# VectorE's mixing operations placed between the masked copies of a scan step, and the state's decay product moved to the middle of the step

## What is computed

```python
sx = concatenate([zeros_like(x[:, :1]), x[:, :-1]], axis=1) - x
m = tanh((x + sx * time_maa_x) @ tm_w1).reshape(Bb, Tt, 5, A)
delta = einsum('btfa,fac->btfc', m, tm_w2)
mix = time_maa_wkvrg[None, None] + delta
xw, xk, xv, xr, xg = [x + sx * mix[:, :, i] for i in range(5)]
...
def step(state, rkvw):
    a = k_t[..., :, None] * v_t[..., None, :]
    y = einsum('bhk,bhkv->bhv', r_t, state + u[None, :, :, None] * a)
    return (w_t[..., :, None] * state + a, y)
...
return yn.reshape(Bb, Tt, Cc) * g @ Wo
```

## Time and profile before

| | us |
|---|---|
| device time, median of 3 runs | 4354.51 (4353.13 to 4363.64) |
| span of the profiled execution, first to last instruction | 4344.3 |
| what lies around the span (median less span) | 10.2 |
| attention | from the start to about 2640 |
| TensorE busy / VectorE busy / ScalarE busy / GpSimd busy | 3769.6 / 3500.5 / 1612.9 / 1139.1 |

### The profile page before, as it was taken

How to read it: one execution, slowest core, us unless ns; L and a number is a source line. 1 busy time by engine, 2 the same in 40 slices (tenths; PEclk the granted TensorE clock), 3 DMA queues, 4 the chain that set the end, 5 groups by cost and what they waited for, 6 DMA issues and landing times. The chain is left out here.

```text
span 4344.3 us, 155632 instructions
## 1 busy us (share of the span) xinstructions
PE 3769.6 (87%) x65992; PEld 2590.6 (60%) x65992; DVE 3500.5 (81%) x7798; ACT 1612.9 (37%) x3173; POOL 1139.1 (26%) x736
## 2 busy tenths in 40 slices
PE   4888898888898888888888874399999999999999
PEld 3767777676677766777767652145454545545454
DVE  4777788777688776778777757799999999999997
ACT  2434434344353443443434313233333333333333
POOL 1121112211212212112121104433333333333332
PEclk7999999999899998999999986599999999999999
DMA  3000000000000000000000011001111111111100
GB/s 112 13 22 27 23 28 18 23 27 18 23 27 23 27 22 19 27 18 33 18 23 27 13 71 66 15 23 37 31 37 35 33 38 30 37 32 36 38 30 30
DMA packets 73617, 133.45 MB, mean 31 GB/s; under 512 B 13248, under 2 KB 14016, under 8 KB 72896
## 3 DMA queue, kind: packets, MB, share of 16 engines
q1 hardware_dynamic: 72896, 123.13, 8.8%
HBM read 89.56 MB, written 33.55 MB: 28 GB/s over the span
## 5 line engine op out<-in xcount | busy, mean ns | idle before, releaser
L747 POOL TENSOR_TENSOR raw_up<-raw_up,raw_gate 128x1024 f32<-128x1024 f32 x128 | 309.8, 2420 | 1184.1 <-DVE raw_up L797 1184.1
L915 DVE COPY_PREDICATED Am<-pick,banks 128x64 f32<-128x64 uint8 (+2 forms) x1792 | 460.6, 257 | 128.3 <-DVE Am L915 12.6
L1630 PE MATMUL fbank<-dT,hqT 128*128 128x512 f16 x2112 | 490.3, 381 | 21.1 <-ACT hqT L1547 21.1
L1618 PE MATMUL fbank<-gT,xqT 128*128 128x464 f16 (+1 forms) x2304 | 490.1, 363 | 11.4 <-issue 6.6
L1618 PE MATMUL fbank<-uT,xqT 128*128 128x464 f16 (+1 forms) x2304 | 488.3, 362 | 0.0
L526 PE MATMUL banks<-raw_up,raw_gate 128*128 128x256 f32 x2048 | 465.8, 386 | 6.2 <-issue 4.4
L526 PEld LDWEIGHTS banks<-raw_up,raw_gate 128*128 128x128 f32 x2048 | 391.0, 193 | 61.0 <-issue 7.0
L758 POOL TENSOR_TENSOR yrs<-yvar,neg_half 128x32 f32<-128x32 f32 x32 | 174.0, 5437 | 846.0 <-DVE yvar L944 846.0
L1618 PEld LDWEIGHTS fbank<-gT,xqT 128*128 128x128 f16 x2304 | 225.3, 98 | 247.7 <-issue 11.5
L1558 ACT ACTIVATE sil<-fbank,und 128x464 f32<-128x464 f32 (+1 forms) x192 | 124.0, 646 | 656.0 <-PE fbank L1618 656.0
L1618 PEld LDWEIGHTS fbank<-uT,xqT 128*128 128x128 f16 x2304 | 225.6, 98 | 231.7 <-issue 1.3
(11 more groups left out here) (235 smaller groups left out, 8063.1 us busy)
## 6 DMA issues: line engine op xcount, KB each, us to landing
raw_scale<-in_L_attn_x SPq DMA_DIRECT2D x32, 512.0 KB, 3.8
xres<-in_L_attn_x SPq DMA_DIRECT2D x32, 512.0 KB, 3.5
x_after_attention<-xres SPq DMA_DIRECT2D x32, 512.0 KB, 3.6
xl<-x_after_attention SPq DMA_DIRECT2D x64, 256.0 KB, 2.7
xr<-x_after_attention SPq DMA_DIRECT2D x64, 256.0 KB, 2.7
out<-xr SPq DMA_DIRECT2D x64, 256.0 KB, 2.0
raw_gate<-in_L_ffn_w_gate SPq DMA_DIRECT2D x1, 2816.0 KB, 11.5
raw_up<-in_L_ffn_w_up SPq DMA_DIRECT2D x1, 2816.0 KB, 18.7
```

The lines of the kernel that those rows point to most:

```text
L747: nc.gpsimd.tensor_tensor(xf[:, j % NXF].rearrange("p g b t -> p (g b) t"), xf[:, j % NXF].rearrange("p g b t -> p (g b) t"), hT[:, :, :, ...
L915: nc.vector.copy_predicated(dst, mask, src).then_inc((done or A_step).sem, 1)
L1618: last = nc.tensor.matmul(GU[2 * pair + t][:, 0:w], xqT[:, u, a, g, :], W[:, b_, g, lo_:hi_], start=(k == 0), stop=(k == 3 * G - 1))
L1630: last = nc.tensor.matmul(DN[1 - u][:], hqT[:, a, kk, :], dT[:, b_, kk, :], start=(first and kk == 0), stop=(end and kk == KF - 1))
```

## The change

Two things are done to VectorE's instructions of a scan step.

1. The four mixing operations of steps 1 to 5, which stood together behind the seven masked copies, now stand one by one inside the step: the first behind the fourth copy, the second behind the update of the state, the third behind the sixth copy, the last behind the seventh. The waits of the mixing (for `delta` and for a free `xf`) stand ahead of the first of them, so inside the step. What followed the four (for `j = 0` the addition of `hT`) is now `dve_mix_end`, and it is called ahead of `dve_z`; before, `dve_z` stood ahead of the whole mixing.
2. The product `s_tmp = state * decay` moves from behind the diagonal product to behind the third copy, in all eight steps.

```diff
-        def dve_mix(dve, i, j):
-            after(dve, delta_done, i, j + 1)
...
+        def dve_mix(dve, i, j, g):
+            if g == 0:
+                after(dve, delta_done, i, j + 1)
...
+            part = nc.vector.scalar_tensor_tensor(xf[:, j % NXF, g], PROJ[g // 2][:, (g % 2) * BT:(g % 2 + 1) * BT].rearrange("p (b t) -> p b t", b=B),
+                                                  col_maa[:, ORDER[j], g:g + 1], sx[:, g], ALU.add, ALU.mult)
+            if g == G - 1:
+                part.then_inc(mixed.sem, 1)
+
+        def dve_mix_end(dve, i, j):
             if j == 0:
                 after(dve, mixed, i, 1)
...
-        def dve_A(dve, c, n):
+        def dve_A(dve, c, n, mix):
...
+            level(16, 4, M1, M2)
+            level(16, 8, M2, M3)
+            level(16, 12, M3, X0)
             if q == 0:
                 after(dve, state_done, c - 1, 4 * b + 4)
             else:
                 after(dve, state_done, c, n)
             nc.vector.tensor_tensor(s_tmp[:], state[:, b, q], t32, ALU.mult).then_inc(s_step.sem, 1)
...
             level(32, 16, X0, SEND)
+            mix(0)
             level(4, 1, S1, S2)
             after(dve, s_step, c, n + 1)
             nc.vector.tensor_tensor(state[:, b, (q + 1) % Q], s_tmp[:], SC[n % 2][:, G * NS:G * NS + G * K].rearrange("p (g v) -> p g v", g=G), ALU.add).then_inc(state_done.sem, 1)
+            mix(1)
             level(4, 2, S2, S3)
+            mix(2)
             level(4, 3, S3, M1, A_done)
+            mix(3)
...
                 if do_w:
-                    dve_A(dve, c, n)
+                    dve_A(dve, c, n, mix)
...
+                if 1 <= n <= 5 and do_p:
+                    dve_mix_end(dve, i, n - 1)
                 if n == 1 and do_f:
                     dve_z(dve, f)
...
-                if 1 <= n <= 5 and do_p:
-                    dve_mix(dve, i, n - 1)
```

More of the change, by code:

```diff
@@ L788, in dve_m @@
             nc.vector.tensor_tensor(m_part[1][:, 1, 0:QT], m_full[:, 1, 0:QT], m_hi[:, 1, 0:QT], ALU.subtract).then_inc(m_done.sem, 1)
-        def dve_mix(dve, i, j):
-            after(dve, delta_done, i, j + 1)
[L792 to L799, removed]
+        def dve_mix(dve, i, j, g):
+            if g == 0:
+                after(dve, delta_done, i, j + 1)
+                if j == 0:
+                    after(dve, td1_done, i - 1)
+                else:
+                    after(dve, proj_done, i - 1, 2 * j)
+            part = nc.vector.scalar_tensor_tensor(xf[:, j % NXF, g], PROJ[g // 2][:, (g % 2) * BT:(g % 2 + 1) * BT].rearrange("p (b t) -> p b t", b=B),
[3 more added lines that the diff above has]
+        def dve_mix_end(dve, i, j):
             if j == 0:
@@ L904, in dve_A @@
             t32 = T32[:].rearrange("p (g x) -> p g x", g=G)[:, :, xb:xb + 1].to_broadcast([P, G, K])
[L905 to L909, removed]
             step = [1]
@@ L927, in dve_A @@
             level(16, 12, M3, X0)
+            if q == 0:
+                after(dve, state_done, c - 1, 4 * b + 4)
+            else:
+                after(dve, state_done, c, n)
+            nc.vector.tensor_tensor(s_tmp[:], state[:, b, q], t32, ALU.mult).then_inc(s_step.sem, 1)
             level(32, 16, X0, SEND)
+            mix(0)
             level(4, 1, S1, S2)
@@ L968, in dve_body, with mix @@
             for n in range(8):
+                def mix(g):
+                    if 1 <= n <= 5 and do_p:
+                        dve_mix(dve, i, n - 1, g)
                 if do_w:
-                    dve_A(dve, c, n)
+                    dve_A(dve, c, n, mix)
+                else:
+                    for g in range(G):
+                        mix(g)
+                if 1 <= n <= 5 and do_p:
+                    dve_mix_end(dve, i, n - 1)
                 if n == 1 and do_f:
```

## The result

The changed kernel takes 4508.07 us (median of 4 runs, 4499.32 to 4514.88) against 4353.82 (4350.05 to 4363.64): 3.66% slower, ratio 1.0366 with a 95% interval of 1.0333 to 1.0399. The forecast was 4495, in a range of 4435 to 4540.

What follows compares the result with a forecast made beforehand. The prediction took TensorE's own stream as the bound, with g(1) repeatedly delayed by another engine. To 4354.5 us it added 105 (chain), 6 (later last copy) and 30 (clock), 141 in all: 4495 us, range 4435 to 4540.

Steps and rivals of the forecast that it cites:

- What bounds the kernel: In the attention TensorE's own stream sets the pace; only at g(1) does another engine repeatedly delay it, 15.7 us in all.
- The chain through `dve_z`: Step 1: `dve_z` behind the mixing makes g(1) start 6.1 us after delta(0) ends, against 2.6; +105 us.
- The later last copy in steps 2 to 5: Last masked copy stands behind three mixing operations, so TensorE's output starts later: +6 us, range 0 to 18.
- The decay product as a cushion: Moved product keeps the last copies of steps 3 and 4 in time; without it 0.5 to 1 us a body lost.
- The clock: g(1)'s products meet TensorE's lower clock after the wait in about two thirds of bodies: +30 us, range 0 to 51.
- the fourth rival: Clock falls in every body and inserted operations cost 0.3 us each: 186 us more, 4540 us; chance 0.18.
- The delay is absorbed: TensorE's "issue" pauses shrink by what g(1) waits, so the time stays at about 4360 us; chance 0.06.
- VectorE as the bound: VectorE sets the pace, so its 2.0 us saved a body count: 4294 us, faster; chance 0.04.
- The signs: If right: `act_gu` waits for `dve_z` in all 30 bodies, TensorE's idle before line 540 exceeds 120 us, g(1)'s clock often below 1.
- The base of the sum: Profiled execution before the change taken as span 4344.3 plus 10.2 around it, 4354.5 us, also the median.

Runs made afterwards that it cites:

- the runs with the link taken away: ScalarE's tanh goes into `yS`, so `act_gu` doesn't wait for `dve_z`: 4334.3 us on the changed kernel, 4331.5 us on the kernel before.
- the kernel with `dve_z` late: Kernel before, with only `dve_z` moved behind the four mixing operations and the addition of `hT` in step 1: 4510.5 us, ratio 1.0371.

## Why the prediction was right

**What bounds the kernel**: right in what matters. TensorE's own stream does. g(1) isn't the only place, though, where another engine makes TensorE late again and again: the scores of a body's first step wait for VectorE's transposed `kT`, and cost more in all than g(1) did before. First before, then changed:

```profile
PE banks L445 <- DVE kT L889: 22.4, 30, 0.7
```

```profile
PE banks L445 <- DVE kT L892: 20.2, 27, 0.7
```

It is 0.75 us each in both, so it has no part in the difference. The change took 80 us of busy time off VectorE and gained nothing by it; the runs with the link taken away repeat that with 101 us.

**The chain through `dve_z`**: right, step by step. The sum was 6.1 us, measured 5.93. The difference lies in the four inserted operations: I took 0.80 us, and the body shown has mixing start to addition start 708.87 - 706.59 = 2.28 against 1.69, so 0.59. Times 30 it was 105 us forecast and 100 measured. The 0.28 for each by the rule of the Trainium skill ("VectorE: DVE Perf Modes", section "The DRAIN you can't avoid") is about twice what the trace has: behind an inserted operation the next one starts 0.09 to 0.20 later. The prediction took half of that section: it also says that a next operation that isn't held starts earlier, and with that the rows agree.

**The later last copy in steps 2 to 5**: the mechanism was there, and its cost at the low end of the 0 to 18 us. TensorE waited 23.4 us for the copies. The kernel with `dve_z` ahead of the mixing shows no cost that can be measured (ratio 0.9985 to 1.0011), since pauses for "issue" shrank by nearly as much. I had 6 us.

**The decay product as a cushion**: wrong. 15 to 30 us were to be lost without it, 4 were measured.

**The clock**: right in kind, the mis-sized term. I forecast the lower level in two thirds of the bodies at 1.35 to 1.7 us, 30 us in all, from g(0)'s bursts. Measured: all 30 bodies at 6.06 - 3.89 = 2.17 us, 65 us in all. As to the clock it was the fourth rival that came true, and its 51 us were too few as well. The rows of g(0) come from stretches in which TensorE still did small products; here it did none for 4.3 us. That the empty stretch is what does it is shown by filling it: with products in the wait no g(1) was long, in either kernel, and with the stretch 1.3 us shorter seven of 30 weren't. Whether small products in it would have left g(1) as g(0) was, no run shows.

**What balanced it.** From D of the first full body to D of the last the traces have 2268.3 us before and 2422.5 after, 154.2 more in 29 bodies. The distance takes 97.8 of it and g(1)'s products 62.3; all the rest of the bodies is 5.9 shorter, though the new wait for the copies lies in it. The last g(1) adds another 5, and the stretches ahead of the first body and behind the last g(1) take 7 less, which makes the 153. So distance and clock are the whole loss; the interleaving adds nothing to it.

**The rivals.** "The delay is absorbed" is refuted: g(1)'s wait gave next to no pause back, as the kernel with `dve_z` late shows (5.2 us a body in the three rows, as before). What pauses gave back, they gave to the wait for the copies. The argument against it had a number wrong: the pause of the earlier trace rows begins 682.78 - 679.34 = 3.4 us behind g(1)'s end; 2.9 is where the output begins. VectorE as the bound is refuted by the runs with and without interleaving.

**The signs.** `act_gu` waited for `dve_z` and the distance was near 6.1 in all 30 bodies, and the clock in g(1) was below 1 in all. TensorE's idle time at line 540 stayed below the 120 us named: 105.9 between 200 and 2500 us, 112.3 in all.

**The base of the sum**: I took median less span, 10.2 us, for what lies around the span. The traced execution of the changed kernel took 4499.3 us at a span of 4497.3, so it is 2.0, and by the same 2.0 the traced execution before, 4344.3 of span, lay some 8 us below the median. From there the forecast for a traced execution would have been 4487, against 4499.3. The forecast of the median isn't hurt by it, since it starts from the median before.

**How much of the closeness is luck.** The terms were 105, 6 and 30. Measured were 100 for the chain, 65 for the clock, and -12 for all the rest of the span. The clock term was less than half of what it had to be, and 23 of its missing 35 us were made up for by the other terms' errors. The chain was forecast; that the total came within 13 us was in part luck.

## What to carry to other kernels

When an operation is moved, ask of every operation that now stands behind a wait it didn't stand behind who needs its result, on all engines; here `dve_z` was no part of what the change was about, and its place alone decided the time. Less busy time on an engine was worth nothing here, since TensorE had waited for next to none of its copies, and the list of waits said so in one line. A buffer that two engines take turns in is often the cheaper thing to change than the order: writing the tanh elsewhere removed the chain and gained 17 us over the kernel before, while the interleaving gained none.

## What the runs showed of the hardware

- An empty stretch of 4.3 us on TensorE ahead of a burst of 16 products made them take 6.06 us in place of 3.7, in 30 of 30 bodies. Work that nobody needs in that stretch (480 records in all) put the granted clock back to 1.00 and the burst to 3.70 us, and the medians fell by 68 us (the traced executions by 46). It paid only as long as it fitted the wait; twice as much cost 93 us more by the medians.
- With the empty stretch shorter (4.67 us from delta(0) in place of 5.93) seven of 30 bursts ran at full clock; in the kernel before, with at most 4.10, 28 of 30.
- TensorE's pauses for "issue" lie whole multiples of 256 of its instructions apart (173 of 177 distances). They shrank by 23.2 us when it waited 24.1 us for the masked copies, and hardly by 89.9 us of waits at g(1) (8.5 us a body to 8.3).
- An operation of VectorE that doesn't wait for the one ahead of it started 0.09 to 0.20 us after one that lasts 0.28 or 0.29.
